# Rotation tables of a four-stage network: phases and whole turns on ScalarE, reduction in place on VectorE, three of the four tables within the first tile

## The reference, cut to what matters

```python
def _lrpe(x, theta, offset=0):
    n = x.shape[-2]
    index = (jnp.arange(n, dtype=x.dtype) + offset).reshape(1, n, 1)
    th = theta * index
    return jnp.concatenate([x * jnp.cos(th), x * jnp.sin(th)], axis=-1)
...
q = _lrpe(q, theta, offset=0)
k = _lrpe(k, theta, offset=0)
y = _lightning_attn(q, k, v, slopes)
```

## Time and profile before

| what | before |
|---|---|
| median of three runs | 1597.89 us (1595.07 to 1600.05) |
| the profiled execution's own time | 1596.48 us |
| its span | 1594.6 us |
| TensorE matmul busy | 1452.9 us, 91% of the span |
| VectorE busy | 957.7 us, 60% |
| ScalarE busy | 724.6 us, 45% |
| GpSimd busy | 776.0 us, 49% |
| mean granted TensorE clock | 0.957 |

### The profile page before, as it was taken

The page is one execution under the profiler, slowest core; times in us unless marked ns, Lnnn a source line. Parts: engine busy times, 40 slices in busy tenths (PEclk is TensorE's granted clock), DMA queues, the critical chain, the costliest instruction groups (busy, mean ns, idle before and its releaser), DMA issues.

```text
span 1594.6 us, 33497 instructions
## 1 busy us (share of the span) xinstructions
PE 1452.9 (91%) x11190; PEld 821.9 (52%) x11191; DVE 957.7 (60%) x1875; ACT 724.6 (45%) x1313; POOL 776.0 (49%) x699
## 2 busy tenths in 40 slices
PE   6889999999999999999998458999999999999980
PEld 3456666644444444445454315666666666666650
DVE  8677777786766666633988883444444444444435
ACT  5344344465464545444445442444444444444433
POOL 3455445540020202044446536777766776777755
PEclk9899999999999999999999568999999999999995
DMA  6222211169776767531101444888888888776559
GB/s 241 90 84 71 74 26 26 38 232 321 240 260 228 260 220 266 194 129 53 55 3 53 155 166 91 180 190 168 204 170 202 193 191 189 148 116 90 72 79 322
DMA packets 102703, 242.84 MB, mean 152 GB/s; under 512 B 21577, under 2 KB 23017, under 8 KB 101616
## 3 DMA queue, kind: packets, MB, share of 16 engines
q1 hardware_dynamic: 67024, 182.47, 34.3%
q0 software_dynamic: 35616, 59.58, 22.4%
HBM read 158.83 MB, written 101.19 MB: 163 GB/s over the span
## 4 chain that ended last, share of the span: by engine, by line
PE 68%; DVE 15%; issue 6%; POOL 5%; ACT 3%; DMA 2%; SPq 1%; DVEq 0%; POOLq 0%; ACTq 0%
PE bank L896 20%; PE bank L917 11%; PE bank L565 8%; PE bank L709 6%; PE bank L715 6%; PE bank L738 6%; PE bank L887 5%; PE bank L906 2%; DVE ARENA L1046 1%; POOL ARENA L1693 1%; ACT ARENA L1410 1%; POOL ARENA L1688 1%; DVE ARENA L1284 1%; PE bank L554 1%; PE bank L818 1%
## 5 line engine op out<-in xcount | busy, mean ns | idle before, releaser
L896 PE MATMUL bank<-ARENA,XT 128*128 x1908 | 364.3, 327 | 2.0 <-DVE XT L1374 1.0
L1822 POOL DMA_INDIRECT acc<-X,WA x159 | 252.4, 1587 | 94.6 <-issue 41.6
L896 PEld LDWEIGHTS bank<-ARENA,XT 128*128 128x128 f16 x1908 | 180.5, 98 | 124.1 <-issue 7.3
L1374 DVE COPY XT<-bank 128x1024 f16<-128x1024 f16 x159 | 109.9, 691 | 183.0 <-PE bank L887 181.9
L1815 POOL DMA_INDIRECT XT<-x_rows,WA x159 | 165.8, 1043 | 91.9 <-DVE XT L1384 35.7
L1410 ACT ACTIVATE ARENA<-ARENA 128x512 f16<-128x512 f32 (+2 forms) x128 | 89.3, 709 | 247.1 <-DVE ARENA L1132 134.2
L917 PE MATMUL bank<-ARENA,XT 128*128 x795 | 197.4, 379 | 0.4 <-issue 0.3
L1647 ACT ACTIVATE XT<-bank 128x192 f32<-128x192 f32 x159 | 52.5, 330 | 289.5 <-PE bank L896 289.5
L565 PE MATMUL bank<-XT,STG 128*128 128x512 f16 x640 | 153.2, 388 | 4.6 <-DVE ARENA L1178 4.3
L565 PE MATMUL bank<-WA,XT 128*128 128x512 f16 (+1 forms) x732 | 133.0, 336 | 13.0 <-DVE ARENA L1028 12.1
L1675 POOL TENSOR_TENSOR rstd<-mv,mhalf 128x1 f32<-128x1 f32 x28 | 8.7, 309 | 258.0 <-DVE mv L965 258.0
(11 more groups left out here) (235 smaller groups left out, 2402.7 us busy)
## 6 DMA issues: line engine op xcount, KB each, us to landing
w_scratch<-WA SPq DMA_DIRECT2D x64, 640.0 KB, 3.9
ARENA<-w_scratch SPq DMA_DIRECT2D x64, 640.0 KB
ARENA<-w_exp SPq DMA_DIRECT2D x48, 640.0 KB, 5.1
WA<-w_exp SPq DMA_DIRECT2D x16, 640.0 KB, 5.0
ARENA<-ARENA SPq DMA_DIRECT2D x64, 128.0 KB, 2.3
acc<-ARENA SPq DMA_DIRECT2D x18, 256.0 KB, 3.3
X<-x SPq DMA_DIRECT2D x4, 1024.0 KB, 6.8
ARENA<-wc SPq DMA_DIRECT2D x8, 512.0 KB, 5.9
```

Of the source, the lines that this page charges most:

```text
L896: mm = pe.matmul(d, xTb[k.u % 2][:, a * KD + kd, :], weights(sl, b, kd * 2 * DFF, 2 * DFF), start=(a, b, kd) == (0, 0, 0), stop=(a, b, kd) ...
L1374: dve.tensor_copy(xTb[k.u % 2].rearrange("p c n -> p (c n)"), bank[k.u % 2][:, :].bitcast(F16)).then_inc(xt_sb, 1)
L1822: pool.indirect_dma_start(acc[i % 2], bass.IndirectOffsetOnAxis(blkidx[:, i:i + 1], 0), yD[i % 8], None, compute_op=ALU.add).then_inc(y_ou ...
```

## The change

Three things are changed together. First, phases and whole turns move from VectorE to ScalarE: `turns(c)` is now three activations (a copy with a scale for each partition, then two identities whose bias is plus and minus the large number, read from two new columns of `mhalf` that GpSimd sets). They write the phases into `cosT` and the turns into `sinT`. VectorE's `angles(c)` keeps three subtractions and the clamp, in place in the tables, and the scratch tiles are gone. In place means that ScalarE's three sine steps each wait for the one before. Second, the work is made earlier: slices 0 and 1 before the first rotation, slice 2 right behind the k rotation of tile 0, and only the subtraction and the sines of slice 3 in tile 1. Nothing is left in tile 2. Third, things around it shift: ScalarE takes pieces 7 to 9 before the state copy of tile 0 and not behind it, VectorE takes piece 8 between the evacuations of tile 0 and piece 9 between the q and k rotations of tile 1, the semaphores of the pieces are reused, and the loads of pieces 8 to 15 each wait on SyncE for the splits of the pieces whose semaphore they take over.

```diff
         def landed(n):
-            i = n if n < LATE else n - LATE
-            if 4 <= n < 8:
-                return wp_raw[n - 4], 16
-            return w_raw[i if i < 6 else i - 4], 16 * (n // LATE + 1)
+            return (wp_raw[n - 4], 16) if 4 <= n < 8 else (w_raw[n % 4], 16 * (n // 4 if n >= 8 else 1))
...
             def load_piece(n):
-                if n >= LATE:
-                    before = n - LATE
+                for before in {8: (0,), 9: (1,), 10: (0, 2), 11: (1, 3), 12: (2, 8), 13: (3, 9), 14: (4, 10), 15: (5, 11)}.get(n, ()):
...
-            def phases(c):
-                own.did(dve.tensor_scalar(ths[c % 2], theta, nidx[:, c:c + 1], None, ALU.mult))
...
-            def turns(c):
-                own.did(dve.tensor_scalar(kk, ths[c % 2], 1 / (2 * np.pi), MAGIC, ALU.mult, ALU.add))
-                own.settle()
-                own.did(dve.tensor_scalar(kk, kk, MAGIC, None, ALU.subtract))
-                own.settle()
-
             def angles(c):
...
+                dve.wait_ge(th_made, 3 * c + 3)
+                th, kk = cosT[:, c, :], sinT[:, c, :]
+                for part in TWO_PI:
+                    own.did(dve.scalar_tensor_tensor(th, kk, -part, th, ALU.mult, ALU.add))
                     own.settle()
-                dve.tensor_scalar(rr, rr, PI_MAX, -PI_MAX, ALU.min, ALU.max).then_inc(th_ready, 1)
+                dve.tensor_scalar(kk, th, PI_MAX, -PI_MAX, ALU.min, ALU.max).then_inc(th_ready, 1)
...
             angles(0)
             split_piece(1)
             split_piece(2)
-            phases(1)
-            turns(1)
+            angles(1)
             split_piece(3)
             split_piece(4)
...
             rotate(0, 1)
+            angles(2)
             dve.wait_ge(d_const, 16 * 4)
...
                 evacuate(t, 1)
                 if first:
-                    angles(1)
+                    split_piece(8)
...
                 if first:
-                    phases(2)
-                    phases(3)
-                    split_piece(8)
-                    split_piece(9)
-                elif isinstance(t, int) and t < TB - 1:
-                    turns(t + 1)
-                    angles(t + 1)
...
+                if isinstance(t, int) and t == 1:
+                    angles(3)
...
                     rotate(t + 1, 0)
+                    if first:
+                        split_piece(9)
                     rotate(t + 1, 1)
...
+            def turns(c):
+                act.activation(cosT[:, c, :], theta, ACT.Copy, scale=nidx[:, c:c + 1]).then_inc(th_made, 1)
+                act.wait_ge(th_made, 3 * c + 1)
+                act.activation(sinT[:, c, :], cosT[:, c, :], ACT.Identity, scale=1 / (2 * np.pi), bias=mhalf[:, 3:4]).then_inc(th_made, 1)
+                act.wait_ge(th_made, 3 * c + 2)
+                act.activation(sinT[:, c, :], sinT[:, c, :], ACT.Identity, bias=mhalf[:, 4:5]).then_inc(th_made, 1)
```

More of the change, by code:

```diff
@@ L103, in build @@
         rstd = sb("rstd", [P, TB, 3], F32)
-        mhalf = sb("mhalf", [P, 3], F32)
+        mhalf = sb("mhalf", [P, 5], F32)
         idle = sb("idle", [P, 1], F32)
@@ L143, in build @@
         Sd = r.take([HEADS, P], F32)
-        th, rr, kk, theta = (r.take([DIM], F32) for _ in range(4))
-        th3 = r.take([DIM], F32)
-        ths = [th, th3]
+        theta = r.take([DIM], F32)
         PAIRS = HEADS // 2
@@ L1002, in _ @@
             dve.memset(stateL, 0.0).then_inc(state_lo, 1)
-            dve.wait_ge(consts_in, 16 * 2)
-            phases(0)
-            turns(0)
             angles(0)
@@ L1418, in xt_copy @@
                      src[:, :].bitcast(F16).rearrange("p (c n) -> p c n", c=2 * KD)).then_inc(xt_new, 1)
+            def turns(c):
[4 more added lines that the diff above has]
+                act.activation(sinT[:, c, :], sinT[:, c, :], ACT.Identity, bias=mhalf[:, 4:5]).then_inc(th_made, 1)
             def sines(c):
                 act.wait_ge(th_ready, c + 1)
[L1422 to L1429 removed]
+                act.activation(cosT[:, c, :], sinT[:, c, :], ACT.Abs).then_inc(sin_done, 1)
+                act.wait_ge(sin_done, 3 * c + 1)
+                act.activation(sinT[:, c, :], sinT[:, c, :], ACT.Sin).then_inc(sin_done, 1)
+                act.wait_ge(sin_done, 3 * c + 2)
+                act.activation(cosT[:, c, :], cosT[:, c, :], ACT.Sin, scale=-1.0, bias=mhalf[:, 2:3]).then_inc(sin_done, 1)
+            act.wait_ge(g_step, 5)
+            act.activation(warm[:, :], mhalf[:, 0:1], ACT.Sin)
+            act.wait_ge(consts_in, 16 * 2)
+            turns(0)
+            hi_piece(0)
+            turns(1)
+            for n in range(1, 3):
                 hi_piece(n)
@@ L1452, in _ @@
             q_high(0)
+            turns(2)
             k_high(0)
@@ L1461, in attention @@
                 if first:
+                    for n in range(7, LATE):
+                        hi_piece(n)
                     sines(1)
@@ L1467, in attention @@
                 copy(stateH, state).then_inc(state_hi, 1)
-                if first:
-                    for n in range(7, LATE):
-                        hi_piece(n)
                 if not first:
@@ L1475, in attention @@
                     hi_piece(LATE + t)
-                if isinstance(t, int) and 1 <= t < TB - 1:
-                    sines(t + 1)
+                if first:
+                    sines(2)
+                    turns(3)
+                if isinstance(t, int) and t == 1:
+                    sines(3)
                 if last:
@@ L1697, in _ @@
             own.did(pool.memset(mhalf[:, 2:3], float(np.pi / 2)))
+            own.did(pool.memset(mhalf[:, 3:4], MAGIC))
+            own.did(pool.memset(mhalf[:, 4:5], -MAGIC))
             own.settle()
```

18 lines of the change are left out of this document (3 added, 15 removed).

## The result

| what | before | with the change |
|---|---|---|
| median of six runs | 1596.48 us (1593.79 to 1600.05) | 1589.46 us (1587.94 to 1590.88) |
| span of the profiled execution | 1594.6 us | 1586.3 us |
| its own time | 1596.48 us | 1588.15 us |
| TensorE matmul busy | 1452.9 us | 1445.6 us, 91% |
| VectorE busy | 957.7 us | 954.0 us, 60% |

The ratio of the times is 0.9953, with a 95% interval of 0.9937 to 0.9970: 7.0 us less in the medians. The forecast was 1589.6.

The account below looks back on a forecast made before the run. The prediction took the ends of the first attention tiles, with TensorE idling for VectorE's q rotation, as the bound. Tiles 0 to 2 sum to -8.3 us: 1588.2 against the profiled 1596.5, plus 1.4 for the median, 1589.6; range 1584 to 1596.

Parts of the forecast that it names:

- What bounds, and the sum: First three attention tiles: their ends bound the gain; +0.1, -3.3 and -5.1 us sum to -8.3.
- Time won here is won at the end: Everything behind tile 3 waits on this stage and is unchanged, so time won here was taken as won at the end.
- The start: Before tile 0: TensorE starts 0.4 us later, at 11.45; q and k rotations come about 1.5 us late.
- Tile 0: Slice 2's instructions take turns with GpSimd, scores start 6.7 us later, the V wait goes; net +0.1 us.
- SyncE's waits: Loads of pieces 8 and 9 wait for splits done at 10.1 and 12.0 us; claimed to cost nothing.
- Tile 1: Tile 1: turns, cosine wait and idle time before V shrink, against a later k rotation; -3.3 us in all.
- the first three terms: In tile 1: turns gone -1.0 us, cosine made long before -1.5, clock holding for V -1.7.
- piece 9's split now holds back the k rotation: In tile 1: the split (1.2 us) delays k, and GpSimd's half of k then meets VectorE's output half; +0.9 us.
- Tile 2: Tile 2: no table left, 24.05 becomes 18.15 us, less 0.8 for a late k chain; -5.1 us.
- the 0.8 (a late k chain): In tile 2: an estimated 0.8 us lost because the k chain is still late from tile 1 and meets VectorE again.
- mild: Rival: milder turn-taking of VectorE and GpSimd in tile 0, 3.7 us better, 1585.9 us; chance 0.17.
- the clock falls anyway: Rival: clock low for twelve more matmuls in tile 0 (2.5 us) and tile 1 (1.7), 1593.8 us; chance 0.16.

Follow-up runs that it names:

- e5: The order of the change alone, with phases and turns made by VectorE again, against the changed kernel: 1595.66 us, ratio 1.0001 to the kernel before.
- r1: The changed kernel itself, unaltered, run and profiled once more: 1589.29 us, ratio 0.9950 to the kernel before.
- e6: The changed kernel with the piece semaphores of before, so loads of pieces 8 and 9 do not wait for earlier splits: 1589.84 us.
- e3: The changed kernel with piece 9's split moved from between tile 1's rotations to behind piece 8's split in tile 0: 1588.61 us.
- e1: The changed kernel with slice 2's four VectorE instructions moved behind tile 0's first evacuation: 1591.12 us, ratio 0.9966 to the kernel before.
- v1: The changed kernel with slice 1's reduction behind tile 0's last evacuation, slices 2 and 3 between evacuations of tiles 1 and 2: 1591.12 us.
- v2: The changed kernel with slice 1's reduction between tile 0's evacuations, piece 8 behind `stateL`, slices 2 and 3 between evacuations of tiles 1 and 2: 1587.64 us.
- v3: As v2, but slices 2 and 3's reductions cut in two around the tile boundary, and piece 9's split beside piece 8's: 1585.27 us, ratio 0.9922.
- e4: The change's move of phases and turns to ScalarE alone, in the order of before: 1594.81 us, ratio 0.9993 to the kernel before.
- r2: The same kernel as v2, run and profiled once more: 1588.13 us, ratio 0.9946 to the kernel before.

## Why the prediction was right, by its own steps

- **What bounds, and the sum.** -8.3 was forecast; the tile ends give -8.66, the span -8.3, the medians -7.0. That the median itself came within 0.2 us of the forecast's 1589.6 is partly luck: the forecast counted from a median of three runs of before, 1597.89, which became 1596.48 with six. "Time won here is won at the end" held for this kernel, whose remainder is 0.4 from that of before. As a rule it is wrong: e5 won 5.7 us in these tiles and kept 2.5 of it in its profiled span and 0.2 in the medians.
- **The start.** TensorE starts at 11.27 (forecast 11.45), the first clamp ends at 10.70 (10.8), the q rotation starts at 17.66 (17.9) and the k rotation ends at 22.41 (22.6). The turn-taking there came as worked out: three subtractions in 3.95.
- **Tile 0.** The clamp was to end at 31.0 and ended at 30.89. The Trainium skill (SBUF — State Buffer, Who interferes with whom) has the exclusive lock, and the trace agrees: 6.26 for 2.14. Scores at 34.48 were forecast for 35.1, +6.1 and not +6.7. The step took the start of the scores before, 28.41, for the landing of the last swap, and so 2.2 us from the end of its issue. In both traces a swap lands 2.4 us after the start of its issue at the latest: at 28.0 before, where the scores stood behind the product for the running state (line 639, until 28.47), and at 34.4 with the change, 1.8 after the end of its issue. There that product (line 633, until 34.44) ends at the same time, so the two waits tie; in r1 TensorE idles 0.16 us between it and the scores. V was to start 9.9 us behind the scores and starts 10.7 behind them, at 45.21 and not 45.0, with no idle time: the 10.0 of before was mis-sized for a clock that now stays low up to 38.4, through most of the scores. The two errors, -0.6 and +0.8, nearly cancel, which is luck. Tile 0: +0.30 against +0.1. ScalarE's last step for slice 3 ended at 43.33 (43.5 forecast; the steps are six, not five), and it then idled 0.27 us for the q rotation: covered, by no more than that.
- **SyncE's waits**: nothing that shows, by e6, a single run.
- **Tile 1.** -3.97 against -3.3. The idle time before V fell from 4.11 to 1.62 (1.7 forecast) and the clock held, 4.45 to 2.76: together -4.2, as the first three terms have it. The term that failed is +0.9, "piece 9's split now holds back the k rotation". It measured 0.2. The split stands there, but with it moved away tile 1 takes the same 20.25 us, and VectorE waits for the k projection instead (e3): the k rotation had slack. The meeting that the step foresaw did take place, as VectorE's low half of the output (line 1081) took 2.21 us where it took 1.01 before, and the evacuation behind it was 0.6 late, but TensorE was in the output projection then and waited for neither.
- **Tile 2.** -4.98 against -5.1: the size is right, the reason given for the 0.8 (a late k chain) is not. The tile pays 0.93 over tile 3, all of it ahead of its first transposes, which wait for GpSimd's low half of q. That the two sizes agree is luck.
- **Rivals.** The collision was not mild, and the clock fell only under the scores. The rival "the clock falls anyway" put twelve cold projections into tile 0; e1 and v1, with one profile each, show how near that was: a fall a few microseconds later costs 1.9 and 1.7 us in 24 projections, and in the change only 0.5 us lay between the clock's return and the projections, in e3 nothing (5.38 us for the 24).
- **The range** rested on the spread of the runs and on tile 0's clock. It left out the joints of the layers, where the same kernel can lose 2.4 us. It held all the same.

## What to carry to other kernels

When two engines exclude each other, moving one of them a few instructions along can simply move the collision (6.26 us in the change, 6.07 in e1 and v2): ask which pause TensorE takes instead. Here the pause was cheaper ahead of short matmuls than ahead of the long stream, by a margin of half a microsecond. A block of dependent instructions can be cut: laid in two places, it gave the shortest first four tiles of all kernels here (v3). And judge a local gain by local times (here the tile ends) as well as by the end, because later joints can give back a few microseconds or hold on to them.

## What the hardware showed that I had not expected

- The length of an idle time alone did not decide the clock. In e4 a wait of 2.48 us was followed by twelve matmuls in 4.26 us and one of 3.31 by twelve in 2.76, and one of 3.33 by 4.42. In e5 2.54 was followed by 2.76. I had taken 4.1 us to cost and short waits to be free. In v3, 2.26 us in the scores cost nothing. The Trainium skill (TensorE: Matmul & The Clock Gate, HAM oscillation) puts it down to idle gaps; its part on the gate (What's actually happening) adds that the activity window runs freely and does not start with the kernel. The second fits v2 and r2, one kernel whose clock fell at the joint in one execution and not in the other; no run here tests it.
- The same four instructions of VectorE beside GpSimd took 8.53 us in the change (22.33 to 30.89, less a gap) and 6.5 in e1 and v2, against 2.6 alone. In e1 and v2 GpSimd had nothing left to do when the clamp came, and it took 0.43 us instead of 2.27.
